# Expert overflow in halves of 64 slots, two experts at a time on the two column halves of TensorE

## What is computed

```python
scores = x @ gate_w.T
mult, sel = _masked_sampling_omp(scores)          # two experts of 8 for each token, with weights
h = silu(einsum('th,efh->etf', x, w1)) * einsum('th,efh->etf', x, w3)     # F = 512
y = einsum('etf,ehf->eth', h, w2)
coef = (one_hot(sel, 8) * mult[..., None]).sum(axis=1)
out = einsum('te,eth->th', coef, y)
x = x + tanh(g_ffn[1]) * out
```

## Time and profile before

| | us |
|---|---|
| median of 3 runs | 232.21 |
| lowest, highest | 231.79, 232.42 |
| the profiled execution | 231.6 |
| its span in the trace | 229.87 |
| PE busy | 212.2 (92%) |
| DVE, ACT, POOL busy | 125.9, 87.1, 86.6 |

### The profile page before, as it was taken

The page is one execution under the profiler, slowest core; times in us unless marked ns, Lnnn a source line. Parts: engine busy times, 40 slices in busy tenths (PEclk is TensorE's granted clock), DMA queues, the critical chain, the costliest instruction groups (busy, mean ns, idle before and its releaser), DMA issues.

```text
span 229.9 us, 3859 instructions
## 1 busy us (share of the span) xinstructions
PE 212.2 (92%) x1272; PEld 165.2 (72%) x1273; DVE 125.9 (55%) x445; ACT 87.1 (38%) x193; POOL 86.6 (38%) x112
## 2 busy tenths in 40 slices
PE   8999989999999989989899999999999999999810
PEld 7796743356864467889799899999999976666510
DVE  3796897999979789978874957211111111111100
ACT  2866655984005460333612722222222223232300
POOL 8347229210011200537323344444763234455540
PEclk9999999999999999999999999999999999999985
DMA  6867044089992157162502313232312311221000
GB/s 178 223 219 233 29 156 157 23 324 414 411 408 89 54 193 304 47 224 86 166 14 29 43 22 62 46 48 38 57 48 26 43 22 22 27 26 10 4 7 3
DMA packets 17049, 26.04 MB, mean 113 GB/s; under 512 B 4350, under 2 KB 12677, under 8 KB 17030
## 3 DMA queue, kind: packets, MB, share of 16 engines
q1 hardware_dynamic: 11328, 20.14, 24.6%
q0 software_dynamic: 4320, 5.25, 13.0%
q10 hardware_dynamic: 1382, 0.41, 0.9%
HBM read 21.34 MB, written 5.77 MB: 118 GB/s over the span
## 4 chain that ended last, share of the span: by engine, by line
PE 51%; DVE 28%; ACT 6%; issue 5%; POOL 2%; DMA 2%; DVEq 1%; POOLq 0%; ACTq 0%
PE PS L1974 20%; PE PS L1998 10%; PE PS L2004 7%; PE PS L1675 3%; PE PS L2018 3%; DVE stat L1001 3%; DVE hT L1393 3%; ACT a L790 2%; PE PS L1960 2%; PE PS L1739 2%; DVE work L1079 1%; DVE x L1253 1%; DMA out_dram<-a,sidx 1%; DVE mv L1008 1%; DVE work L1065 1%
## 5 line engine op out<-in xcount | busy, mean ns | idle before, releaser
L1974 PE MATMUL PS<-hT,e 128*128 128x128 f32 x480 | 58.9, 276 | 1.1 <-ACT hT L914 0.6
L1974 PEld LDWEIGHTS PS<-hT,e 128*128 128x128 f32 x480 | 56.8, 192 | 2.5 <-ACT hT L914 1.2
L1641 DVE TENSOR_TENSOR hT<-th,PS 128x512 f32<-128x512 f32 x20 | 13.7, 686 | 63.6 <-PE PS L1974 38.1
L1857 PE MATMUL PS<-xnT,e 128*128 128x512 f32 x88 | 39.6, 598 | 2.0 <-DVE hT L1393 0.9
L1857 PEld LDWEIGHTS PS<-xnT,e 128*128 128x128 f32 x88 | 16.1, 190 | 22.2 <-issue 17.4
L1998 PE MATMUL PS<-e,hT 128*128 128x256 f32 x120 | 28.6, 381 | 0.2 <-DVE x L1431 0.2
L1998 PEld LDWEIGHTS PS<-e,hT 128*128 128x128 f32 x120 | 21.7, 190 | 3.2 <-issue 0.8
L604 POOL TENSOR_TENSOR rstd<-veps,nhalf 128x2 f32<-128x2 f32 x12 | 8.7, 728 | 39.1 <-DVE veps L1010 39.1
L665 POOL DMA_INDIRECT out_dram<-a,ids_early x8 | 12.8, 1596 | 26.5 <-ACT a L943 14.5
L1871 PE MATMUL PS<-e,hT 128*128 128x256 f32 x96 | 21.7, 383 | 0.0
L924 ACT ACTIVATE th<-PS 128x512 f32<-128x512 f32 x20 | 11.9, 594 | 22.5 <-PE PS L1974 15.2
(11 more groups left out here) (276 smaller groups left out, 331.7 us busy)
## 6 DMA issues: line engine op xcount, KB each, us to landing
e<-e_in SPq DMA_DIRECT2D x24, 512.0 KB, 8.2
x<-x_in SPq DMA_DIRECT2D x2, 512.0 KB, 6.2
graph_rows<-e SPq DMA_DIRECT2D x4, 256.0 KB, 2.4
out_dram<-x SPq DMA_DIRECT2D x4, 256.0 KB, 2.5
xn_rows<-xn SPq DMA_DIRECT2D x4, 256.0 KB, 2.4
e<-gw_in SPq DMA_DIRECT2D x1, 768.0 KB
e<-uw_in SPq DMA_DIRECT2D x1, 640.0 KB
e<-dw_in SPq DMA_DIRECT2D x1, 640.0 KB
```

The lines of the kernel that those rows point to most:

```text
L1641: dve.tensor_tensor(hh[me], th[:, me, :], PS[:, 2 + me, :], ALU.mult).then_inc(gated, 1)
L1857: mm = pe.matmul(PS[:, bank, :], w[:, k, it * P:(it + 1) * P], xnT[:, h, k, :], start=(k == 0), stop=(k == 1))
L1974: mm = pe.matmul(PS[:, bank + q, f * P:(f + 1) * P], w[:, k * F + f * P:k * F + (f + 1) * P], xgT[q][:, k, :], start=(k == 0), stop=(k == 1))
```

## The change

The late overflow is counted in halves of 64 slots, not in blocks of 128. Four halves are served by two static *packs*, at j = 13 and 14 of a program of 18 blocks (blocks 15 to 17 are the ordinary late blocks of experts 6, 7 and 0). In a pack, slots 0 to 63 belong to one expert and slots 64 to 127 to another (or the same), and each matmul is done as two of 64 stationary columns: the first writes PSUM partitions 0 to 63, the second 64 to 127, from different weights. Only from the fifth half on does a loop run, over two packs at a time.

- SP loads the weights of the four halves from DRAM again, by a row number read at run time (12 DMAs of 512 KB), over the weights of experts 1 to 4, whose late blocks are 8 to 11, as soon as these have used them (`staged`).
- A token may be in both halves of one pack. Then its two rows would be added by one scatter at once. So DVE and PE (`same_rows`, `spread_rows`) build a 0/1 matrix of equal row numbers, `merge` multiplies the pack's scaled output with it, so that both rows hold the sum, ACT copies it (`copy_merged`), and the second of two equal row numbers is set out of bounds.
- The lists have 20 columns, not 24; `nb`, `ehalf` and `eoff` have more entries, for halves.
- On POOL the three last gathers and the scatters of late blocks stand in another order.

The core of the diff:

```diff
-STATIC = 2 * E - 1
-
-OVER = 14
-NO = OVER + 2
+PACKS = (E + 5, E + 6)
+STATIC = 2 * E + len(PACKS)
+
+
+HALF = P // 2
+NH = 24
+NO = NH // 2
 NL = E + NO
+MOST = 6 * 2
...
                       ("gather_rows", 3), ("norm_var", 2), ("norm_var", 3),
                       ("attn_stats", 0), ("attn_stats", 1), ("moe_stats", 0), ("moe_stats", 1),
...
         def pairs_in_use(engine):
 
             engine.wait_ge(blocks_ready, 1)
-            return engine.value_load(blocks[0:1, 1:2], min_val=0, max_val=OVER // 2)
+            return engine.value_load(blocks[0:1, 1:2], min_val=0, max_val=(NH - 1) // 4)
 
         def place(j):
 
             if j < E:
                 return 0, EARLY[j]
-            return 1, j - E
+            if j in PACKS:
+                return 1, E + PACKS.index(j)
+            return 1, j - E - (len(PACKS) if j > PACKS[-1] else 0)
...
+            def row_of(half):
+                return sp.value_load(eoff[0:1, half], min_val=0, max_val=(E - 1) * P)
+
+            def stage(w, src, cols, row, signal):
+                sp.dma_start(w[:, cols], src.rearrange("e p n -> (e p) n")[bass.ds(row, P), :]).then_inc(signal, 16)
+
+            sp.wait_ge(eoff_ready, 1)
+            for p in range(len(PACKS)):
+                for n in range(2):
+                    cols, free, row = staged_in(p)[n], freed_by(p)[n], row_of(slice(2 * p + n, 2 * p + n + 1))
+                    sp.wait_ge(up1_done, free + 1)
+                    stage(e1, e1_in, cols, row, staged[p])
+                    sp.wait_ge(up3_done, free + 1)
+                    stage(e3, e3_in, cols, row, staged[p])
+                    sp.wait_ge(y_done, free + 1)
+                    stage(e2, e2_in, cols, row, staged[p])
+            pairs = pairs_in_use(sp)
...
+                rows_to = ids[h][:, at:at + 1]
+                if j in PACKS:
+                    p = PACKS.index(j)
+                    rows_to = pack_ids[:, p:p + 1]
+                    pool.wait_ge(same_ready, 1)
+                    pool.wait_ge(merged, p + 1)
+                else:
+                    pool.wait_ge(y_scaled, j + 1)
...
+                if j in PACKS:
+                    to = raw[PACKS.index(j)]
+                elif j >= E:
+
+                    act.wait_ge(scattered, 16 * (j - E + 1))
+                act.activation(to, PS[:, Y_BANK, (j % 2) * C:(j % 2 + 1) * C], copy,
                                scale=coef[h][:, at:at + 1]).then_inc(y_scaled, 1)
...
+            def copy_merged(p):
+
+                act.wait_ge(merge_done, p + 1)
+                act.wait_ge(scattered, 16 * (PACKS[p] - E + 1))
+                act.activation(yv[kept_in(PACKS[p])], PS[:, 7, p * C:(p + 1) * C], copy).then_inc(merged, 1)
...
+            for j in range(7, STATIC + 2):
+                if j < STATIC:
+                    silu(j)
+                if j - 1 in PACKS:
+                    copy_hhT(PACKS.index(j - 1), (j - 1) % 2)
+                if j - 2 in PACKS:
+                    copy_merged(PACKS.index(j - 2))
+                if j + 1 < STATIC:
+                    copy_x(j + 1)
+                if j <= STATIC:
+                    scale_y(j - 1)
             pairs = pairs_in_use(act)
...
                 dve.tensor_tensor(column[:, 1], slot[:, 1], iota_c[:, :].unsqueeze(2).to_broadcast([P, E, HT]), ALU.add)
                 own(dve.tensor_tensor(left[:, :], spare[:, :], tally[:, 1, :, HT], ALU.add))
-                own(dve.tensor_tensor(nb[:, :, :], left[:, :].unsqueeze(2).to_broadcast([P, E, E - 2]),
-                                      iota_q[:, 1:E - 1].unsqueeze(1).to_broadcast([P, E, E - 2]), ALU.is_gt))
+                own(dve.tensor_tensor(nb[:, :, :], left[:, :].unsqueeze(2).to_broadcast([P, E, MOST]),
+                                      iota_h[:, :].unsqueeze(1).to_broadcast([P, E, MOST]), ALU.is_gt))
...
-                own(dve.scalar_tensor_tensor(out=base[:, :], in0=base[:, :], scalar=float(P), in1=iota_w[:, :],
+                own(dve.scalar_tensor_tensor(out=base[:, :], in0=base[:, :], scalar=float(HALF), in1=iota_w[:, :],
                                              op0=ALU.mult, op1=ALU.add))
...
+                own(dve.tensor_tensor(ehalf[:, :, :], iota_b[:, :].unsqueeze(2).to_broadcast([P, NH, E]),
+                                      incl[:, :].unsqueeze(1).to_broadcast([P, NH, E]), ALU.is_ge))
+                own(dve.tensor_reduce(eblk[:, :], ehalf[:, :, :], AX.X, ALU.add))
+                dve.tensor_scalar(eoff[:, :], eblk[:, :], float(E - 1), float(P), ALU.min, ALU.mult).then_inc(eoff_ready, 1)
+                own(dve.tensor_scalar(blocks[:, 0:1], incl[:, E - 1:E], 1.0, -1.0, ALU.max, ALU.add))
+                dve.tensor_scalar(blocks[:, 1:2], blocks[:, 0:1], 2, None, ALU.logical_shift_right).then_inc(blocks_ready, 1)
...
+            def same_rows(h):
+
+                dve.wait_ge(list_ready, 2)
+                for p in range(len(PACKS)):
+                    ins = dve.tensor_scalar(same[p][:, 0:P], ident[:, :], pack_row[:, p:p + 1], None, ALU.mult)
+                ins.then_inc(row_numbers, 1)
+                for p in range(len(PACKS)):
+                    dve.wait_ge(rows_spread, 1)
+                    n = mark(dve.tensor_scalar(same[p][:, P:2 * P], PS[:, 7, p * P:(p + 1) * P], pack_row[:, p:p + 1], None, ALU.is_equal))
+                after(n)
+                for p in range(len(PACKS)):
+                    n = mark(dve.tensor_reduce(twice[:, p:p + 1], same[p][:, P:P + HALF], AX.X, ALU.max))
+                after(n)
+                own(dve.tensor_scalar(twice[:, :], twice[:, :], later_half[:, 0:1], None, ALU.mult))
+                dve.tensor_tensor(pack_ids[:, :], pack_row[:, :], twice[:, :], ALU.add).then_inc(same_ready, 1)
 
...
+            def up_pack(w, bank, q, p, ready):
+
+                a, b = staged_in(p)
                 for k in range(2):
-                    mm = pe.matmul(PS[:, bank + q, :], xgT[q][:, k, :], w[:, bass.ds(at + k * F, F)],
-                                   start=(k == 0), stop=(k == 1))
+                    for n, cols in enumerate((a, b)):
+                        half_of = slice(n * HALF, (n + 1) * HALF)
+                        mm = pe.matmul(PS[half_of, bank + q, :], xgT[q][:, k, half_of], w[:, cols][:, k * F:(k + 1) * F],
+                                       start=(k == 0), stop=(k == 1))
                 mm.then_inc(ready, 1)
 
...
+            def spread_rows(h):
+
+                pe.wait_ge(row_numbers, 1)
+                for p in range(len(PACKS)):
+                    mm = pe.matmul(PS[:, 7, p * P:(p + 1) * P], ones[:, :], same[p][:, 0:P], start=True, stop=True)
+                mm.then_inc(rows_spread, 1)
+
+            def merge(p):
+
+                pe.wait_ge(y_scaled, PACKS[p] + 1)
+                pe.wait_ge(same_ready, 1)
+                pe.matmul(PS[:, 7, p * C:(p + 1) * C], same[p][:, P:2 * P], raw[p], start=True, stop=True).then_inc(merge_done, 1)
 
...
-                up1(j)
+            for j in range(7, STATIC + 2):
+                if j in PACKS:
+                    p = PACKS.index(j)
+                    pe.wait_ge(xgT_copied, j + 1)
+                    pe.wait_ge(gated, j - 1)
+                    pe.wait_ge(staged[p], 16 * 6)
+                    up_pack(e1, 0, j % 2, p, up1_done)
+                elif j < STATIC:
+                    up1(j)
                 if j == 7:
                     block_list(3)
-                turn_x(j + 1)
-                up3(j)
-                down(j - 1)
-
-            pe.wait_ge(eoff_ready, 1)
-            pe.wait_ge(coef_ready, 2)
-            pe.wait_ge(xgT_copied, STATIC + 1)
-            pe.wait_ge(gated, STATIC - 1)
-            up_over(e1, 0, 1, 0, up1_done)
-            turn_x_over(STATIC + 1, 0, 0, 16 * 3)
-            up_over(e3, 2, 1, 0, up3_done)
-            down(STATIC - 1)
+                if j == 9:
+                    spread_rows(0)
+                if j - 1 in PACKS:
+                    if j - 1 == PACKS[0]:
+                        pe.wait_ge(coef_ready, 2)
+                    turn_h(j - 1, (j - 1) % 2)
+                if j - 2 in PACKS:
+                    merge(PACKS.index(j - 2))
+                if j + 1 < STATIC:
+                    turn_x(j + 1)
+                if j in PACKS:
+                    up_pack(e3, 2, j % 2, p, up3_done)
+                elif j < STATIC:
+                    up3(j)
+                if j - 1 in PACKS:
+                    down_pack(j - 1, PACKS.index(j - 1), (j - 1) % 2, PACKS.index(j - 1))
+                elif j <= STATIC:
+                    down(j - 1)
             pairs = pairs_in_use(pe)
             with pe.Fori(0, pairs) as i:
                 for q in range(2):
```

219 lines of the change are left out of this document (111 added, 108 removed).

## The result

| | before | after |
|---|---|---|
| median of the runs, us | 232.31 (4 runs, 231.79 to 232.97) | 274.99 (4 runs, 273.9 to 275.8) |
| profiled execution, us | 231.6 | 273.9 |
| its span, us | 229.87 | 271.9 |
| mean granted clock of TensorE | 0.985 | 0.933 |

After takes 1.183 times as long as before (95% interval 1.178 to 1.188). It is slower by 43 us where the prediction said 8 us faster, and it lies far outside the range. The page of the kernel after shows at a glance where: busy shares and the granted clock in 40 slices, and GB/s, which answer to the earlier trace rows.

The account below looks back on a forecast made before the run. PE bounds the kernel until the tail; it ends 9.5 us earlier, at 210.0, but chained scatters leave 7.9 saved: 231.6 - 7.9 = 223.7 profiled, with the median 0.6 above, about 224.4 us; range 222.5 to 225.8.

Parts of the forecast that it names:

- so the loop runs zero times: Overflow loop: four halves of 64 fill exactly the two static packs, so no pass of the loop; two passes before.
- Halves side by side: Packs on PE: column halves overlap, an up 1.72 us and a down 1.73, as for one expert.
- the switches: PE entering and leaving tiles in the packs: five stretches of 0.28 us, 1.4 us; bounds 0 and 2.8.
- Rival 1: Packs on PE: column halves run one after the other, 10.3 us more on PE, 234.6 us; chance 0.16.
- rival 2: Packs on PE: halves overlap but in program order of passes, an up 2.15 us, 226.5 us; chance 0.10.
- rival 3: Packs on PE: a half's weights load only while the other stands still, 4.2 us, 228.6 us; chance 0.08.
- From the first pack to PE's end: PE from iteration 13 through the last down: 33.0 us, ending at 210.0 us, 9.5 us earlier.
- Ahead of it: PE before iteration 13: `spread_rows` adds 0.44 us, gate 8 a wait of 0.2 to 0.3; PE 0.6 us late.
- The last down waits for ACT: PE's last down waits 0.8 us for ACT's copy of the down before it, both in bank 6.
- The tail: Scatters 14 to 17 run one after another, 4.5 us for a full one; last starts at 213.3; 7.9 us saved.
- rival 4: Second pack on PE: pack 1 waits 2.2 us for its weights, 226.6 us; chance 0.06.
- A sign of being wrong that came true: POOL's scatters: the forecast is wrong if they come over 5 us apart under the weight loads.

Follow-up runs that it names:

- e2: The changed kernel with each engine's loop under a test of its count, entered only if not zero: 224.21 us (0.963 of before).
- e1: The changed kernel with the loops of all five engines left out: 224.06 us (0.963 of before).
- e7: The changed kernel with SP's loop of weight loads and PE's wait for them left out, the empty pass still running: 267.2 us.
- e10: On top of e1, each pack's matmuls have all 128 columns and the weights of its first half alone: 222.84 us.
- e3: On top of e1, the 12 weight loads of the static packs and PE's wait for them left out: 223.91 us.
- e4: On top of e2, `spread_rows` one iteration earlier, behind block 8 instead of block 9: 223.46 us.
- e8: On top of e1, all matmuls of a pack's first half ahead of those of the second: 226.35 us (0.976 of before).
- e9: On top of e4, second merge and its copy ahead of block 16's up, late downs ahead of up3: 222.75 us (0.959 of before).
- e11: On top of e1, the two merges and their copies left out, packs' scaled outputs scattered directly: 224.23 us.

## Why the prediction was wrong

**The step that failed** is the sentence "so the loop runs zero times", and the one that closed the rivals: a loop that still runs "can't" with four halves counted, "and I give it no share of its own". The counting was right (e2: the count on the chip is zero). What was never looked up is what a loop does with a count of zero. The order of PE's instructions in the built program holds the answer, and it could have been read before any run:

```
L480 TENSOR_LOAD blocks [waits blocks_ready]
L480 ISA x2
...
L2161 UNCONDITIONAL_BRANCH
L2161 ISA
...
L2161 REGISTER_ALU
L2161 COMPARE_AND_BRANCH
```

The branch into the body is unconditional and the only comparison stands behind the body. The kernel before gave no hint, because its count was two. "18 gate operations on DVE, not 20" was the observation that would show it, and showed it: x20.

**Where the pass's 51 us go.** POOL's timeline has the last static scatter:

```profile
217.18 1.55 POOL L732 DMA_INDIRECT out_dram<-a,ids_late  x1 [5.47 <-DMA out_dram<-a,ids_late]
```

Scatter 17 starts at 217.18 us, against 214.08 in e1. Of these 3.1 us, 2.5 come from the landing of scatter 16, 6.24 against 3.76 us, under the loop's weight loads; by the other 0.6 scatter 16 itself started later. From there to the last scatter, at 264.30, are 47.1 us. Together 50.2, against 50.9 between the medians. The windows of after show what is busy (start:end, length, busy us of PE, PEld, DVE, ACT and POOL, granted clock, DMA share, GB/s):

```profile
190.00:211.00 21.00, 20.34 (x153) 17.89 (x150) 2.07 (x3) 5.28 (x12) 7.21 (x6) 1.00 0.20 26
211.00:225.00 14.00, 0.45 (x3) 0.05 (x1) 0.00 (x0) 0.47 (x1) 3.97 (x8) 0.65 1.03 371
225.00:237.00 12.00, 9.46 (x38) 3.48 (x38) 0.69 (x1) 1.58 (x3) 0.00 (x0) 0.70 0.26 108
```

Little overlaps. From 211 to 225 us PE is busy for 0.45 us, while weights and rows come in; from 225 to 237 PE works, POOL is idle and the last of the weights land. PE's timeline has the two waits (in brackets: idle before, and what ended it):

```profile
225.52 0.68 PE L2167 MATMUL PS<-ident,sim 128*128 128x128 f32 x2 [14.07 <-DMA sim<-xn_rows,gidx]
...
248.91 0.69 PE L2167 MATMUL PS<-ident,sim 128*128 128x128 f32 x2 [11.66 <-DMA sim<-xn_rows,gidx]
```

PE stops at 211.45 us. Its granted clock is still 1.00 from 212 to 214 us and 0.50 from 216 on, its lower level, 1.2 GHz. It is still there when the first pack's ups begin (same columns as above):

```profile
226.70:229.00 2.30, 2.30 (x6) 0.74 (x8) 0.00 (x0) 0.00 (x0) 0.00 (x0) 0.50 0.62 253
```

From 233.2 to 237 us it is 1.00 again, and after the next idle stretch 0.50 from 249 to 252. That fits the time of a pack's two ups, 6.44 and 5.00 us, where two ups of a static pack take 3.74: 4.0 us in all. The weight loads are not the reason, since the two take 5.16 and 6.05 us without them (e7). A pack of the loop takes about 22 us (first scatters at 238.84 and 260.78), against 5.8 us for a block of the pipelined loop before, which has one scatter and no weights to load.

**The other steps,** with the pass taken away (e1) or from the static part of after, held as mechanisms; some were mis-sized:

- *Halves side by side.* Forecast 1.72 us an up and 1.73 a down, plus the switches; measured 1.87 and 1.73 to 1.88. Two halves gave 3.44 / 1.87 = 1.84 times the speed of one after the other, 92% of two, so the later time by 2.7 us that the prediction worked out from 79% did not come. Rival 1 (3.4 us) is out. PE's timeline of after has two first passes together, which answers to the earlier trace rows:

```profile
178.28 0.65 PE L2086 MATMUL PS<-e,hT 128*64 128x512 f32 x2
...
178.28 1.08 PE L2086 MATMUL PS<-e,hT 128*64 128x512 f32 x4
```

  Two passes are through in 0.65 us and four in 1.08, not in 0.86 and 1.72 plus a drain. This excludes rival 2, which wanted 2.15 us for an up.
- *Weight loads of the halves.* A load of 64 columns takes 132 ns at least and 137 in the median, as rival 3 said, but beside passes in flight: the 32 slots of that rival would have shown 4.2 us, and e10 shows 1.2 to 1.4 for everything that the column form costs. The Trainium skill's rule behind that rival (TensorE: Matmul & The Clock Gate, The mechanism: a load overlaps matmuls in flight only where the row group differs) does not hold for these halves, which share all rows. The page of the kernel before already spoke against it: an ordinary up of 1.78 us holds 16 loads of 128 columns, with a mean of 0.19 us each (L1974), 3.1 us together.

```profile
L2086 PEld LDWEIGHTS PS<-e,hT x64: 132/137/230, 178.3 to 254.0; 128*64 128x64 f32 x64
```

- *From the first pack to PE's end.* The forecast put iteration 13 at 177.0 us and PE's end at 210.0, 33.0 us later. In e1 they are at 177.73 and 210.84 (208.87 + 1.97): 33.1 us.
- *Ahead of it* was mis-sized. The forecast had PE 0.6 us late at iteration 13; it is 1.3 us late in e1 (177.73 against 176.42) and 1.9 in after. Part of it is the wait for gate 8, for which the forecast took 0.2 to 0.3 us, from DVE steps of 1.2 us. DVE's and PE's timeline of after:

```profile
157.66 0.61 DVE L1714 TENSOR_SCALAR work<-PS,pack_row 128x128 f32<-128x128 f32 x2 [8.30 <-PE PS L2111]
...
159.06 1.40 DVE L1725 TENSOR_TENSOR hT<-th,PS 128x512 f32<-128x512 f32 x2
...
159.80 1.99 PE L2076 MATMUL PS<-e,hT 128*128 128x256 f32 x8 [0.17 <-DVE hT L1725]
```

  The steps took 1.4 us (157.66 to 159.06). PE's own wait is short, 0.17 us, but the down behind it takes 1.99 us and not 1.73. With `spread_rows` iteration 9 is 0.89 us longer than before in e1, where the forecast had 0.6 to 0.7. The rest was there when iteration 9 began, 0.4 us in e1 and 1.0 in after; one execution of each cannot say whether it is a cost of the change. It is also why the DVE steps began 0.9 us later than forecast (156.75).
- *The last down waits for ACT.* Forecast 0.8 us, measured 0.66. PE's timeline of e1, which answers to the earlier trace rows:

```profile
208.87 1.97 PE L2019 MATMUL PS<-e,hT 128*128 128x256 f32 x8 [0.66 <-ACT a L964]
```

- *The tail.* Forecast scatters 14 to 17 at 199.9, 204.2, 208.8 and 213.3 us. POOL's timeline of e1, which answers to the earlier trace rows:

```profile
200.50 1.55 POOL L722 DMA_INDIRECT out_dram<-a,pack_ids  x1 [4.67 <-ACT a L971]
...
209.55 1.54 POOL L722 DMA_INDIRECT out_dram<-a,ids_late  x1 [3.55 <-ACT a L964]
...
214.08 1.54 POOL L722 DMA_INDIRECT out_dram<-a,ids_late  x1 [3.00 <-DMA out_dram<-a,ids_late]
```

  Scatter 15 starts at 204.45. They are 0.3 to 0.8 us late, which is the 0.7 us by which iteration 13 is late and what lies around it. The last two stand 4.5 us apart, the later one behind a DMA, as forecast. The end behind the last scatter was mis-sized the other way: the forecast put it at 8.15 + 0.5 us, for a scatter with full rows, and it took 7.9 (214.08 to 222.0).
- *The second loading* (rival 4) costs nothing that can be measured in e1 (e3), and PE does not wait for it there. But the forecast's 3 to 4 us for the critical load was too little: from the end of the down that frees its buffer to the landing it took 6.04 us in e4 and 5.79 in e10, and PE waited for it, 0.17 and 0.58 us. The room was 0.6 us in e1 and not the 2 or 3 that the forecast had.
- *A sign of being wrong that came true.* The forecast was to be wrong if scatters came over 5 us apart under the loads. They did: those at 162.62, 170.38, 176.84 and 184.43 us in e1 stand 7.8, 6.5 and 7.6 us apart, and 5.4 to 6.0 in e3 without the loads. It cost e1 nothing in the end: the first pack's scatter, at 194.26 us, waits for ACT's copy of the merge, as the forecast had said of it. The sign was too strict.

So with the pass taken away the time is 224.06 us, against a forecast of 224.4. Part of this agreement is luck: the last scatter starts 0.8 us later than forecast, and the end behind it is 0.7 us shorter. The packs, the order and the tail were right as mechanisms. The error of 51 us was one assumption about control flow that no term of the sum tested.

## What to carry to other kernels

A static path that takes the work out of a run-time loop saves nothing until the loop itself is skipped: look in the built program at where the comparison stands, and put a test of the count around a loop that may run zero times (0.15 us here, less than the runs' spread, against 51). An estimate that rests on "this does not run" needs the same evidence as one that rests on a duration. And a body that is written as a rare fallback, with gather, up, down and scatter one after another, must be priced as if it ran: 22 us a pack here, against 5.8 us for a block where the next one's steps are issued ahead and no weights are loaded.

## What the runs showed of the hardware that was not expected

- A loop whose count is zero on the chip ran its body once (274.99 us with count 0, 275.33 with count 1, 224.21 with a test of the count).
- Two matmuls on different column halves of the same rows run side by side even with f32 passes and different weights (an up of both halves in 1.87 us, one after the other it would be 3.44), and the weight loads of both lie beside passes in flight.
- Written one half behind the other, the second half began when four passes of the first were left: at once with four passes a half (1.87 us in e8), and only in the fifth slot with eight (2.63 and 2.79 us against 1.73 and 1.88). Alternating the halves keeps both busy.
- A scatter whose rows are all out of bounds still costs 2.70 to 2.75 us to its landing in the loop (from 237 us to the end of after all DMAs together move 0.01 MB), against 3.23 to 3.83 for the others in undisturbed places above.
- The gather of an empty pack beside the 12 weight loads took 5.29 us, and 2.24 to 2.25 without them; a full scatter there 6.24 us, and 3.76 without.
- Two scatters landed in 4.95 us (e9) and 5.01 us (e11) with no weight load near, where their like takes 3.6 to 3.8. In the DMA records of both traces a fetch of 16 KB of instructions starts while the scatter's packets move (at 204.83 and 211.38 us), and these packets are spread over 2.4 and 2.5 us, where those of the same scatters in e1 take 1.3. In e4 such a fetch falls between the packets of two scatters (209.26 us), and both land in time (3.62 and 3.73 us). With two cases this is a coincidence worth a look and not shown.
